# A graph and expert network on one core: four clears with a repeated source, key rows first, and the second edge list and unit lists inside the first graph layer's program

## The reference

```python
    x = x + _L0_gnn_ref(_layernorm(x, axis=-1), src, dst, edge_weight, ...)
    ...
    # in _L0_gnn_ref(x, rows, cols, edge_vals, ...); called with rows = src, cols = dst
        gathered = edge_vals[:, None] * x[cols]
        new_x = jax.ops.segment_sum(gathered, rows, num_segments=N_NODES)
        out1 = new_x @ hamilton1
```

## Time and profile before

| what | value |
| --- | --- |
| median of 3 runs | 2825.48 us (2815.58 to 2832.08) |
| the profiled execution | 2822.73 us |
| its span | 2820.9 us, 49472 instructions |
| granted TensorE clock, mean over the span | 0.847 |
| DMA | 381.37 MB, mean 135 GB/s |

### The profile page before, as it was taken

One profiled execution on the slowest core, in us unless ns is written; L12 is line 12 of the kernel. 1 busy time (PEld: TensorE's weight loads), 2 busy tenths in 40 slices (PEclk: granted clock), 3 DMA queues, 4 the chain that ended last, 5 costly groups with the idle time before them and its releaser, 6 DMA issues. The chain is left out here.

```text
span 2820.9 us, 49472 instructions
## 1 busy us (share of the span) xinstructions
PE 2125.6 (75%) x10310; PEld 1616.9 (57%) x10311; DVE 1787.4 (63%) x4382; ACT 1123.3 (40%) x2764; POOL 1529.9 (54%) x1278
## 2 busy tenths in 40 slices
PE   4587777877776278999996767777777775679990
PEld 2465555655554156777784435555555554569990
DVE  5466677777668353333535848888888887654436
ACT  0354444444442042222323126666666662213332
POOL 0288888888887201777530037777777770025550
PEclk8677787787777587999997888999999998769995
DMA  7577777778777621232124457676666673532225
GB/s 250 150 111 127 120 128 132 124 126 128 130 119 103 155 66 51 46 75 61 45 77 159 149 169 207 194 203 200 201 196 201 199 197 97 190 125 70 71 67 187
DMA packets 257818, 381.37 MB, mean 135 GB/s; under 512 B 36246, under 2 KB 186181, under 8 KB 257477
## 3 DMA queue, kind: packets, MB, share of 16 engines
q0 software_dynamic: 109808, 194.70, 34.0%
q1 hardware_dynamic: 128021, 155.22, 18.3%
q10 hardware_dynamic: 19904, 30.41, 3.1%
HBM read 264.28 MB, written 115.94 MB: 135 GB/s over the span
## 5 line engine op out<-in xcount | busy, mean ns | idle before, releaser
L1006 POOL DMA_INDIRECT sum_tab<-Vs,spot x416 | 684.6, 1646 | 163.5 <-issue 100.1
L2424 POOL DMA_INDIRECT KV<-kv_tab,iS x448 | 472.6, 1055 | 183.6 <-issue 110.3
L893 PE MATMUL psV<-XN,Bs 128*128 x832 | 327.4, 506 | 167.9 <-issue 149.5
L893 PEld LDWEIGHTS psV<-XN,Bs 128*128 128x128 f32 x832 | 160.2, 233 | 306.1 <-issue 299.9
L2612 PE MATMUL psO<-msg,hot 128*128 128x264 f32 x896 | 228.5, 399 | 77.6 <-DVE agg L2532 56.3
L2600 PE MATMUL psQ<-Qs,hotT 128*128 x904 | 241.5, 414 | 56.2 <-issue 38.7
L972 ACT COPY Vs<-psV 128x512 f32<-128x512 f32 x208 | 121.6, 586 | 296.4 <-DMA sum_tab<-Vs,spot 242.8
L2612 PEld LDWEIGHTS psO<-msg,hot 128*128 128x128 f32 x896 | 165.4, 194 | 129.1 <-issue 104.8
L2600 PEld LDWEIGHTS psQ<-Qs,hotT 128*128 128x128 f32 x904 | 172.4, 203 | 108.8 <-issue 82.1
L1393 POOL DMA_INDIRECT ST<-h_tab,src x192 | 183.9, 958 | 58.5 <-issue 58.5
L2462 DVE TENSOR_TENSOR KV<-KV,psQ 128x1024 f32<-128x1024 f32 x112 | 136.7, 1221 | 77.4 <-issue 36.8
(11 more groups left out here) (592 smaller groups left out, 4380.6 us busy)
## 6 DMA issues: line engine op xcount, KB each, us to landing
kb<-key_rows SPq DMA_DIRECT2D x104, 256.0 KB
lowB<-low_tab SPq DMA_DIRECT2D x30, 512.0 KB
sum_tab<-zeros ACTq DMA_DIRECT2D x52, 256.0 KB, 3.0
parts<-sum_tab SPq DMA_DIRECT2D x20, 640.0 KB
ye_tab<-Ye SPq DMA_DIRECT2D x20, 640.0 KB, 3.5
Y<-ye_tab SPq DMA_DIRECT2D x20, 640.0 KB
lowB<-sort_tab SPq DMA_DIRECT2D x23, 384.0 KB, 6.0
keyB<-sort_tab SPq DMA_DIRECT2D x22, 384.0 KB, 5.3
```

What stands on the lines that cost most here:

```text
L893: ins = nc.tensor.matmul(psV[:, r % 2, x, :], Bs[:, q % 2, 2 * h + x, :], XN[:, bass.ds(t, 1), :].rearrange("p a d -> p (a d)"), start=Tru ...
L1006: pool.indirect_dma_start(out=sum_tabs[k], out_offset=bass.IndirectOffsetOnAxis(ap=spot[:, s, u:u + 1], axis=0), in_=Vs[:, j % VR, :], in_ ...
L2424: pool.indirect_dma_start(out=KV[:, s, u, :], out_offset=None, in_=kv_tab, in_offset=bass.IndirectOffsetOnAxis(ap=iS[:, s, u:u + 1], axis= ...
```

## The change

All of `items_phase` and `sort_start_phase` moves into `gnn0_phase`, which becomes one program; their temporary tables are views of its own buffers, and `psE`, `psU`, `psD` and `psN` views of its psum banks. On each engine:

- ScalarE issues four clears instead of 52, one per table, whose source is `zeros` repeated 13 times per partition; they wait for the first edge list (`e_in`). All five square roots come behind them.
- SP loads both edge lists and x, writes the sort tables and `key_rows`, and then goes straight on with the keys of item groups 0 to 3. The stores of `XN`, the goals, the first sort tables, and the layer's weights follow behind these.
- TensorE makes `psK` ahead of `psI`, and of `psI` the sources first.
- VectorE copies the key rows after four of the five statistics groups, and the sources after the first norm. The four steps of the second list (`list_edges`) and of the unit list (`unit_tiles`, `unit_picks`, `unit_goals`, `unit_ends`) are now in pass 0. The clearing matmul of `psP` waits for the last of them, behind pass 1.

The diff, cut:

```diff
-        act.wait_ge(nulled, 1)
-        for k in range(NTAB):
-            for z in range(ZP):
-                act.dma_start(sum_tabs[k].rearrange("(p z j) f -> p z (j f)", p=P, z=ZP)[:, z, :], zeros[:, :]).then_inc(blank, 16)
-        for g in range(3, NG):
...
+psI, psE = [bank(psV, 1), bank(psV, 0), psP], psL[:, :].rearrange("p (n t) -> p n t", n=2)
+psU, psD, psN = psL, psP, psL
...
@@ -628,18 +361,6 @@
         def sort_lows(k, s):
             sp.dma_start(lowB[:, s, :, :].rearrange("p j e -> p (j e)"),
                          sort_tabs[1][bass.ds(k * JS * P, JS * P)].partition_broadcast(P)).then_inc(lowB_in[s], 16)
...
+        sp.wait_ge(halved, 1)
+        for n in range(2):
+            sp.dma_start(sort_tabs[n][0:E2].rearrange("(b t e) -> t b e", t=TB, e=P), row16[:, n, :, :]).then_inc(s_out, 16)
+            sp.dma_start(sort_tabs[n][E2:(T + MORE) * P].rearrange("(t e) -> t e", e=P), nil16).then_inc(s_out, 16)
+        sp.wait_ge(keys_s, 1)
+        sp.dma_start(key_rows.rearrange("(k p) e -> p k e", p=IB), keyT[0:IB, :, :]).then_inc(k_out, 16)
+        sp.wait_ge(k_out, 16)
+        for m in range(2):
+            for z in range(KZ):
+                keys(m, m, z)
+        ahead(1)
+        for g in range(NG):
+            sp.wait_ge(normed, (g + 1) * GT)
+            sp.dma_start(table_rows(xn_table)[:, group(g), :], XN[:, group(g), :]).then_inc(stored, 16)
+        sp.wait_ge(edged, 1)
+        for n in range(2):
+            at = n * (NU * P + 1)
+            sp.dma_start(goal_rows[at:at + 1].unsqueeze(0), edge[:, n:n + 1]).then_inc(goal_out, 16)
+        sp.wait_ge(goals_s, 1)
+        sp.dma_start(goal_rows[1:1 + NU * P].rearrange("(k p e) -> p k e", p=IU, e=P), goalS[0:IU, :, :]).then_inc(goal_out, 16)
+        sp.wait_ge(goal_out, 48)
+        sp.wait_ge(s_out, 64)
+        for k in range(2):
+            sort_lows(k, k)
+            sort_keys(k, k)
+        for Ht, wd in zip(H, (g0_w1, g0_w2)):
+            for ra in range(4):
+                for cb in range(4):
+                    comp = ra ^ cb
+                    sp.dma_start(Ht[64 * (ra % 2):64 * (ra % 2) + 64, ra // 2, 64 * cb:64 * cb + 64],
+                                 wd[:, 64 * comp:64 * comp + 64]).then_inc(h_in, 16)
+        sp.dma_start(gam[:, :], g0_gamma.rearrange("(m p) -> p m", p=P), allow_slow_non_contiguous=True).then_inc(h_in, 16)
+        sp.dma_start(bet[:, :], g0_beta.rearrange("(m p) -> p m", p=P), allow_slow_non_contiguous=True).then_inc(h_in, 16)
+        for b in range(2, CT + 1):
             ahead(b)
         sp.wait_ge(onesies, 1)
         sort_lows(2, 0)
         with sp.Fori(CT + 1, TRIPS) as b:
             ahead(b)
         sp.wait_ge(built, QG * NGI)
+        sp.wait_ge(stored, 16 * NG)
         for i in range(GI):
             sp.dma_start(wide[8 * i:8 * i + 8, :, :], bass.AP(goal_rows.tensor, i * P, ((0, 8), (GI * P, NGU), (1, P + 2)))).then_inc(wide_in, 16)
...
+        for g in range(4):
+            statistics(g)
+        dve.wait_ge(keys_t, 1)
+        v.tensor_copy(keyT[0:IB, :, :].rearrange("p k e -> p (k e)"), psK[0:IB, :]).then_inc(keys_s, 1)
+        statistics(4)
+        norm(0)
+        dve.wait_ge(sources_s, 1)
+        ce.seq(v.tensor_copy(srcI[:, :], psI[1][:, 0:NI]))
+        ce.seq(v.tensor_scalar(off[:, :], srcI[:, :], spare[:, 0:1], None, ALU.subtract))
+        ce.seq(v.tensor_scalar(srcI[:, :], srcI[:, :], -1.0, None, ALU.mult))
         dve.sem_inc(ready, 1)
-        c.inc(v.memset(zeroh[:, :], 0.0))
-        c.inc(v.memset(resets[:, :, 1:JS + 1], 1.0))
-        c.inc(v.memset(resets[:, :, 0:1], 0.0))
-        dve.wait_ge(iotas, 1)
-        c.seq(v.tensor_copy(iota_h[:, :], iota_i[:, :]))
-        dve.sem_inc(cleared, 1)
+        norm(1)
+        norm(2)
+        dve.wait_ge(items_s, 1)
+        ce.inc(v.scalar_tensor_tensor(dlI[:, :], tile_f, -float(P), psI[0][:, 0:NI], ALU.mult, ALU.add))
+        ce.seq(v.tensor_copy(wI[:, :], psI[2][:, 0:NI]))
+        norm(3)
+        norm(4)
+
+        def list_edges():
+            dve.wait_ge(turned, 1)
+            ce.inc(v.tensor_copy(key2, psE[:, 0, :]))
+            ce.inc(v.tensor_scalar(keyC[:, 0:T], psE[:, 0, :], -float(HALF), None, ALU.add))
+            ce.inc(v.tensor_scalar(carried[:, 0:T], psE[:, 1, :], -float(HALF), None, ALU.add))
+            ce.inc(v.memset(lo[:, T:T + MORE], 0.0))
+            ce.inc(v.memset(hi[:, T:T + MORE], -1.0))
+            ce.inc(v.memset(keyC[:, T:T + MORE], 0.0))
+            ce.seq(v.memset(carried[:, T:T + MORE], 0.0))
+            ce.inc(v.tensor_single_scalar(loi, key2, P - 1, ALU.bitwise_and))
+            ce.seq(v.tensor_single_scalar(hii, key2, 7, ALU.logical_shift_right))
+            ce.inc(v.tensor_copy(lo[:, 0:T], loi))
+            ce.seq(v.tensor_copy(hi[:, 0:T], hii))
...
                 if u % QT == QT - 1:
                     ins.then_inc(weighed, 1)
+            if zero(b) and not s:
+                list_edges()
             hold(dve, ranked, m + 1)
...
             for s in range(2):
                 pairs(b, s)
+                if zero(b) and not s:
+                    unit_tiles()
                 for z in range(CB):
                     tally((2 * b + s) * CB + z, z % 2)
+                    if zero(b) and z == CB // 2:
+                        (unit_picks, unit_goals)[s]()
+            if zero(b):
+                unit_ends()
         loop(dve, CT, counting)
...
+        ins.then_inc(turned, 1)
+        pe.wait_ge(picks, 1)
+        for b in range(4):
+            for k in range(4):
+                ins = nc.tensor.matmul(psK[0:IB, b * P:(b + 1) * P], pick[:, k, b * IB:(b + 1) * IB], rawf[1][:, k, :], start=(k == 0), stop=(k == 3))
+        ins.then_inc(keys_t, 1)
+        for n, done in ((1, sources_s), (0, None), (2, items_s)):
+            for k in range(4):
+                ins = nc.tensor.matmul(psI[n][:, 0:NI], rawf[n][:, k, :], pick[:, k, :], start=(k == 0), stop=(k == 3))
+            if done:
+                ins.then_inc(done, 1)
...
         def batches(b, s, z):
+            if zero(b) and (s, z) == (0, 1):
+                unit_tiles()
+            if zero(b) and (s, z) == (1, 1):
+                unit_rows()
             if z:
                 for n in range((z - 1) * CB // 3, z * CB // 3):
                     tally((2 * b + s) * CB + n, n % 2)
+            if zero(b) and (s, z) == (1, 3):
+                unit_ends()
         loop(pe, CT, lambda b: pairs(b, lambda b, s: None, batches))
         nc.tensor.matmul(psH[:, 0:NH], zeroh[:, 0:P], zeroh[:, 0:NH], start=False, stop=True).then_inc(counted, 1)
+        pe.wait_ge(goals_s, 1)
+        nc.tensor.matmul(psP[:, 0:T], zeroh[:, 0:P], zeroh[:, :], start=True, stop=False)
...
+        act.wait_ge(nulled, 1)
+        act.wait_ge(e_in, 16 * 9)
+        for k in range(NTAB):
+            act.dma_start(sum_tabs[k].rearrange("(p z j) f -> p z (j f)", p=P, z=ZP),
+                          zeros[:, :].unsqueeze(1).broadcast_to([P, ZP, SUM_ROWS // P // ZP * D])).then_inc(blank, 16)
+        for g in range(NG):
+            act.wait_ge(stats, (g + 1) * GT)
...
+        nc.gpsimd.memset(zeros[:, :], 0.0).then_inc(nulled, 1)
+        pool.wait_ge(blank, 16 * NTAB)
...
         XN = keep_sb(g_ctx, "XN0", [P, NT, D])
-        items_phase(srcI, dlI, wI, tile_row, key_rows, nbrU, dlN, tile_u, goal_rows, zeros, XN, xn_tab)
-        sort_start_phase(f0_edges[1, :], f0_edges[0, :], keyC, loC, hiC, carriedC)
-        gnn0_phase(srcI, dlI, wI, tile_row, key_rows, XN, tile_u, goal_rows, H0, gam0, bet0,
+        gnn0_phase(srcI, dlI, wI, tile_row, key_rows, nbrU, dlN, tile_u, goal_rows, zeros, XN, xn_tab, f0_edges, H0, gam0, bet0,
                    keyC, loC, hiC, carriedC, firstC, end2, E2, first2, src2)
     r_ctx = h_ctx
     XNT0 = keep_sb(r_ctx, "XNT0", [P, NG, 2, GT * P])
```

More of the change, by code:

```diff
@@ L620, in keys @@
                                          key_rows[at, :].rearrange("i e -> (i e)").partition_broadcast(P)).then_inc(kb_in[s], 16)
-                        for m in range(2):
-                            for z in range(KZ):
-                                keys(m, m, z)
                         def sort_keys(k, s):
@@ new lines, in norm @@
+                        def norm(g):
+                            dve.wait_ge(rooted, g + 1)
+                            v.reciprocal(rs[:, group(g)], sd[:, group(g)]).then_inc(inverse, 1)
+                            dve.wait_ge(inverse, g + 1)
+                            for t in range(g * GT, (g + 1) * GT):
+                                v.tensor_scalar(XN[:, t, :], X[:, t, :], mv[:, t, 0:1], rs[:, t:t + 1], ALU.subtract, ALU.mult).then_inc(normed, 1)
+                        ce.inc(v.memset(raw[0][:, 3, :], PAD_DST))
```

535 lines of the change are left out of this document (208 added, 327 removed).

## The result

The changed kernel takes **2855.2 us** (median of 4 runs, 2853.3 to 2864.0) against 2824.1 for the kernel before in the same session: ratio 1.0114, 95% interval 1.0096 to 1.0131. It is 31 us slower, where 2783 was forecast, outside the range of 2764 to 2808 and on the other side of no change. Its profiled execution took 2853.3 us, with a span of 2851.5; that of the kernel before had a span of 2820.9.

What follows compares the result with a forecast made beforehand. No engine was busy throughout; GpSimd's 416 scatters paced the changed stage. Starting them at 66 instead of 118 gains 52 us, less 2 + 7 + 1 given back, 42 us: 2783 us forecast, range 2764 to 2808.

Steps and rivals of the forecast that it cites:

- the sum: First graph layer: 52 us gained at the start, 10 given back, so 42 us less for the kernel.
- The stages behind see the same inputs in the same state.: Stages after the first graph layer: assumed unaffected, with no cost charged for them.
- the forecast's own range: Whole kernel: first scatter at 62 with 4 given back (2774) to 70 with 17 (2795); chance 0.69.
- the rivals: Four other outcomes: loads come last (0.12), first passes eat the gain (0.12), slow repeated source (0.03), start stays late (0.04).
- Rival 3: Clears before the first scatter: the repeated source is slow, they end at 154, kernel slower at 2871; chance 0.03.
- Wrong in its core if the first scatter comes early and the last one does not: First graph layer: the sign that would refute the forecast, which expected first scatter 62 to 70, last near 899.
- Start of the chain: Before the first scatter: picks at about 20.5, key rows as first product, first scatter at 66 instead of 118.0.
- the lower bound: Before the first scatter: 19.6 MB must move at 377 GB/s, 52 us from 10, so first scatter at 62.
- Given back: First graph layer's passes: 2 us for added work, 7 for stores, 1 for SP's queue, 10 in all.
- VectorE at 63 to 66 us in pass 0: First pass of scatters: edge and unit list work raises VectorE's busy time from 49.0; 2 us charged.
- The 7 us of the stores: Middle of pass 0: five stores of normed rows (3.2 MB) under scatters cost 7 us, bounds 0 and 11.
- the queue of SP: Group 4's keys, behind goals, tables and weights, land at +81, just in time; 1 us charged, bounds 0 and 8.

Runs made afterwards that it cites:

- 24 pads: Changed kernel with 24 one-element memsets on VectorE ahead of the attention loop: 2788.1 us, ratio 0.9868 to the kernel before.
- 104: Kernel before the change with 104 one-element memsets on VectorE ahead of the attention loop: 2887.1 us, ratio 1.0220.
- the two runs with two clears ahead: Changed kernel plus 24 VectorE memsets, two clears at once; the others after the key rows landed (2779.1 us), or third before the last square root, fourth after (2787.9 us).
- 92 pads before: Kernel before the change with 92 one-element memsets on VectorE ahead of the attention loop: 2822.7 us, ratio 0.9994.

## Why the prediction was wrong, and where it was right

**The step that failed** is a sentence behind the sum: "The stages behind see the same inputs in the same state." The inputs were the same. The state wasn't: every instruction that a change takes out of an engine's program moves all later ones. The text treated code that isn't edited as code that can't change. So what the change costs the later stages stood at nothing; it was 67 us, and that turned the sign. That the position is the cause is shown from both sides (24 pads take the 67 us from the changed kernel, 104 add 63 to the one before); that it is a fourth block which is touched is inferred from the packets and the count, and fits all five positions tried, which are four places in a block. VectorE's other long loop, 267 instructions in the graph layer, touches no fourth block at either place by the same count, and its passes from the third on took 62 us in both kernels. With VectorE's pads alone the same change takes 2788 us, inside the forecast's own range (2774 to 2795) and 5 from its 2783; so the sum was nearly right for the stage it was made for. Part of that is luck: the start gained 43.2 us where 52 was forecast, and 6.9 were given back where 10 was, and the two errors partly cancel (36 us kept against 42).

None of the rivals had this mechanism. Rival 3 had the right side for another reason (the repeated source is slow); the clears landed in 30.7 us by the median on the profile's page, which speaks against it, and with 52 plain clears the time was the same. "Wrong in its core if the first scatter comes early and the last one does not" looked no further than the stage: both came early, and the kernel was slower.

**The Trainium skill**, Runtime: NRT & Kernel Launch, section "Instruction fetch mechanics", would have raised the question: it says that prefetch of instructions is sequential, and that a taken branch whose target isn't at hand holds the engine until it is fetched. The trace agrees, with a stall of 4.4 us at the branch back. The page has the buffer refilled in blocks of 16 KiB, 256 instructions; here the packets on the queue that grew (q14) had 8192 bytes (those of q8, whose count no run changed, had 16384), and the period of 128 in the runs speaks for 128 to a block. By the page's blocks a shift of 128 would have moved the body by half a block, and a stretch of 21 or so bad places can't hold both; the measurement decides.

**Start of the chain.** Forecast: first scatter at 66, with 62 to 80 as bounds; measured 74.8. The term that was mis-sized is the key rows. The text had them through near 42; they were issued at 34.1 but landed only at 47.9, 13.8 us on, and the keys took until 58.5, where 49.7 was forecast (its own terms, 42 + 1.8 + 5.5, add up to 49.3). These small transfers, issued behind the large ones, took longest with all four clears ahead: from the issue of the key rows to their landing it was 13.8 us there, 8.9 with the clears behind x, and 6.7 and 4.3 in the two runs with two clears ahead. The assumption that x and clears share the engines held. But they were full until 59 us, and whatever was asked for late came at the end. The DMA view of 9 to 65 us, in 40 equal slices:

```profile
GB/s 138 100 350 404 399 404 399 396 401 400 399 404 400 403 397 403 402 400 392 393 393 401 397 406 412 402 410 408 411 408 401 309 377 410 404 408 171 16 0 12
```

That is 400 GB/s from 12 to 59 us, where the lower bound had 377. From there the 16.3 us to the first scatter came out exactly (58.54 to 74.79). The last square roots at 40 cost nothing, as said.

**Given back.** Forecast 2 + 7 + 1 = 10; measured 43.2 - 36.3 = 6.9. VectorE at 63 to 66 us in pass 0 was wrong: it was busy 45.1, less than before. Its work did not shrink, it spread out: 8.5 us of it now lie between ScalarE's first square and the first scatter (5.4 before), and passes 0 and 1 together have 88.6 us (86.5 before). Nor did it lengthen the scatters, as the prediction held possible on top of its sum: they were busy 56.2 us in pass 0 (55.8 before). The 7 us of the stores were 1, by the run that moved them. For the queue of SP 1 us was charged with the keys of group 4 at +81; they were asked for at 160.7 and squared only at 169.3 (+94.5), and ScalarE waited 4.6 us for them, but in pass 1 GpSimd waited for ScalarE's copies only 0.9 us in all, so the buffer covered it. What makes up the 6.9 us wasn't traced to one cause: of pass 0, 3.7 us are one wait of GpSimd for older scatters.

**Scatters.** 1647 ns against the 1650 forecast.

## What to carry to other kernels

When a change adds or removes instructions ahead of a loop, look at every later loop with a long body on some engine, where its place decides how many instruction blocks it touches (278 instructions here; by the count of this case one of up to 257 can't touch a fourth block), and compare the instruction queue's packets in the two profiles before believing a difference of a few per cent. An unexplained "issue" time at the first instruction of a loop body, once a turn, is the mark; some cheap instructions ahead of the loop move it out, and a benchmark of an edit should be read with and without them. Before a latency chain starts, order transfers by who waits for them: with 13.6 MB of clears ahead small rows took 14 us to land, with half of them 4 to 7, and the engine that issues the clears can be held (29.8 us by four, 6.2 by two).

## What the runs showed of the hardware

- A loop body of 278 instructions on VectorE cost 5 to 7 us more in each turn at some places of its program than at others: 48.0, 53.3, 55.2 and 48.0 us a turn at four places 12 apart (runs with 92 pads before, no pads, 12 and 24), and 53 again 128 further on.
- The instruction packets were 5 in a slow turn and none in a good one; each was 8192 bytes, and the stall at the branch back was 4.4 us, or 7.2 us with the body 12 places further on.
- 92 and 128 one-element memsets on VectorE ahead of the loop cost nothing that these runs can tell (2822.7 against 2825.6; 2856.0 against 2855.2).
- ScalarE, as an issuer of transfers, was held 29.8 us by four clears of 3.4 MB beside x, 27.5 us by four without x, and 6.2 and 5.1 by two beside x: two were accepted within 6 us, four were not.
- TensorE's granted clock in attention_phase was 0.97 where the loop ran freely and 0.91 where VectorE stalled in each turn, and 0.97 again with 24 pads.
